# Last batch's norm woven into the batch ahead, VectorE for GpSimd at both ends of the second layer, sums on GpSimd in the third

## The reference, cut to what matters

```python
# second layer, end of a batch's block (b, l, e = 8, 256, 512); og is the result of the scan over l
m = og.mean(-1, keepdims=True)                       # per head of 16
va = ((og - m) ** 2).mean(-1, keepdims=True)
og = ((og - m) / jnp.sqrt(va + 1e-05)).reshape(b, l, e) * gn_w + gn_b
x1 = x + og * g @ Wo.T
xc = _ln(x1, ln2_w, ln2_b)
sx2 = jnp.concatenate([state[:, 0:1] - xc[:, :1], xc[:, :-1] - xc[:, 1:]], axis=1)
xk2 = xc + sx2 * ffn_maa_k
xr2 = xc + sx2 * ffn_maa_r
rr = jax.nn.sigmoid(xr2 @ Wfr.T)
kk = jnp.square(jax.nn.relu(xk2 @ Wfk.T))
return x1 + rr * (kk @ Wfv.T)

# third layer: two cross attentions (16 heads of 128), then the feed-forward part
h = _layer_norm(x, ln1_scale, ln1_offset)
x = res + _cross_attention(h, xf_1, wq1, ...)
h = _layer_norm(x, ln2_scale, ln2_offset)
x = res + _cross_attention(h, xf_2, wq2, ...)
h = _layer_norm(x, ln_mlp_scale, ln_mlp_offset)
h = gelu(h @ w_fc1 + b_fc1) @ w_fc2 + b_fc2          # inner width 2048
return x + h
```

## Time and profile before

| | |
|---|---|
| median of 3 runs (lowest to highest) | 4452.52 us (4450.16 to 4452.68) |
| the profiled execution: time, span | 4447.1 us, 4445.4 us |
| busy share of the span | TensorE 94%, VectorE 66%, ScalarE 44%, GpSimd 35% |
| mean granted TensorE clock | 0.98 of full |
| second layer | about 826 to 1829 us |
| third layer | about 1829 to 4366 us |

### The profile page before, as it was taken

One profiled execution on the slowest core, in us unless ns is written; L12 is line 12 of the kernel. 1 busy time (PEld: TensorE's weight loads), 2 busy tenths in 40 slices (PEclk: granted clock), 3 DMA queues, 4 the chain that ended last, 5 costly groups with the idle time before them and its releaser, 6 DMA issues. The chain is left out here.

```text
span 4445.4 us, 70612 instructions
## 1 busy us (share of the span) xinstructions
PE 4173.9 (94%) x22096; PEld 3147.2 (71%) x22096; DVE 2953.5 (66%) x6494; ACT 1964.5 (44%) x3814; POOL 1575.7 (35%) x1082
## 2 busy tenths in 40 slices
PE   7999999678999996699999999999999999999999
PEld 3444444356777774588887797887887977888866
DVE  5666665278888885375774775766776756757743
ACT  3555555222333321355553455552555543555522
POOL 1222333155566653123233333233332334232230
PEclk8999999899999998899999999999999999999999
DMA  1000000300000000222212322222212122222122
GB/s 40 25 22 28 20 20 15 119 5 10 15 15 15 15 10 19 84 63 77 68 58 74 96 65 77 63 72 71 92 59 76 58 73 92 64 86 65 54 79 97
DMA packets 128412, 239.78 MB, mean 54 GB/s; under 512 B 16932, under 2 KB 40100, under 8 KB 126896
## 3 DMA queue, kind: packets, MB, share of 16 engines
q1 hardware_dynamic: 126544, 232.99, 16.4%
q0 software_dynamic: 1008, 3.67, 0.2%
...
## 5 line engine op out<-in xcount | busy, mean ns | idle before, releaser
L1940 POOL TENSOR_TENSOR c_wl<-c_wr,c_wh 128x512 fp32r<-128x512 f32 (+1 forms) x576 | 819.7, 1434 | 1689.6 <-ACT c_wh L2273 1386.9
L2374 ACT ACTIVATE c_pr<-c_ps,c_nms 128x257 f32<-128x257 f32 x512 | 244.1, 477 | 483.8 <-DVE c_nms L2596 481.6
L582 ACT ACTIVATE a_ex<-a_ps 128x1024 f32<-128x1024 f32 x256 | 261.1, 1023 | 259.9 <-PE a_ps L417 259.8
L1529 DVE TENSOR_TENSOR_SCAN b_sb<-b_wt,b_s,b_ps 128x256 f32<-128x256 f32 x512 | 361.6, 736 | 16.3 <-PE b_ps L1072 4.4
L695 DVE TENSOR_REDUCE a_nm<-a_ps 128x2 f32<-128x1024 f32 x256 | 311.4, 1221 | 80.5 <-PE a_ps L394 80.4
L2273 ACT ACTIVATE c_wh<-c_wr 128x512 fp32r<-128x512 f32 (+1 forms) x464 | 315.4, 687 | 47.6 <-PE c_ps L2002 43.9
L1480 POOL TENSOR_TENSOR b_sb<-b_sb,b_rt 128x1024 f32<-128x1024 f32 x128 | 278.0, 2178 | 153.6 <-DVE b_sb L1529 113.3
L2000 PE MATMUL c_ps<-c_hh,c_wh 128*128 128x512 f32 x768 | 310.5, 404 | 12.5 <-DVE c_hl L2480 12.1
L2000 PE MATMUL c_ps<-c_gh,c_wh 128*128 128x512 f32 x768 | 307.5, 400 | 9.6 <-DVE c_gl L2658 4.3
L2002 PE MATMUL c_ps<-c_hh,c_wl 128*128 128x512 f32 x768 | 304.6, 397 | 0.0
L2001 PE MATMUL c_ps<-c_hl,c_wh 128*128 128x512 f32 x768 | 304.0, 396 | 0.0
...
## 6 DMA issues: line engine op xcount, KB each, us to landing
...
c_wr<-in_wk SPq DMA_DIRECT2D x128, 256.0 KB, 2.9
c_wr<-in_wq SPq DMA_DIRECT2D x128, 256.0 KB, 2.6
...
```

Of the source, the lines that this page charges most:

```text
L582: act.activation(EX[:, n % 4, :, :], ps[:, BT + 2 * (n % 2):BT + 2 * (n % 2) + 2, :], ACT.Exp).then_inc(ex_ready, 1)
L1529: mm = dve.tensor_tensor_scan(SB[:, quad % RING, pr % 2, e, 1:L + 1], WT[:, third(b, i), e, :], half(spread_bank(pair), e), S0[:, b % 2, 2 ...
L1940: pool.tensor_tensor(piece(WL, slot), piece(WR, slot), piece(WH, slot), ALU.subtract).then_inc(piece_cut[slot], 1)
L2374: act.activation(PR[:, i, 0:L + 1], ps[:, BS + 1 - i % 2, 0:L + 1], ACT.Exp, bias=NMS[:, i:i + 1], scale=float(K2) ** -0.5, accum_out=RS[: ...
```

## The change

Second layer, start (t = 0): `scale`, `shift` and the first `mix` addition go from GpSimd to VectorE, and `constants()` moves behind the reciprocal and the scaling. Second layer, end: `due_post` takes batch 7 out of `post_stage`, and of batch 6 the second `fr`, both `fv` and `out`. A function `last_stages` on TensorE, ScalarE and VectorE issues them: batch 7's group norm in turns with batch 6's remaining products, pairs in two banks (PA, PF, also GATHER and PB), gate, scaling and shift on VectorE, the residual taken from `XA` in place of a load into `XB`, and the output stored in two halves. Third layer: GpSimd adds the four chunks of x, and of the squares, of the woven norm, and TensorE multiplies the one sum; `variance` moves behind `up` of f=5; two of the down products move from ahead of head 15's scores to behind them.

```diff
         XK, XR, KK, TR, OUT = ZB, SQB, XPB[:, :, 0:L], SXB, ZB
+        ZL, XL = XF[:, 0], XA
         SELF = ZB[:, :, :].rearrange("p a (b m) -> p (a b) m", m=P)
         ps = stack.enter_context(nc.psum_tensor("b_ps", [P, 8, 512], F32))
         SPREAD, GATHER, PF, PA, PB = 0, 4, 5, 6, 7
+        LAST_BANKS, LAST_GATES = (PA, PF), (PB, PA)
 
...
+        def due_post(slot, first, last=B - 2):
+
+            s = due(slot, first)
+            return s if s is not None and s <= last else None
...
-            sp.wait_ge(out_stored, B * 16 + AHEAD)
+                    if post < B - 1:
+                        sp.dma_start(XB[:, :, :], x1T[post]).then_inc(res_in, 16)
+            for i in range(2):
+                pair = slice(2 * i, 2 * i + 2)
+                sp.wait_ge(out_ready, B + i + AHEAD)
+                sp.dma_start(x2T[B - 1][:, pair, :], OUT[:, pair, :]).then_inc(out_stored, 16)
+            sp.wait_ge(out_stored, (B + 1) * 16 + AHEAD)
...
-                    s = due(slot, PE_AT["gm"][i])
+                    s = due_post(slot, PE_AT["gm"][i])
...
-                    s = due(slot, PE_AT["fr"][i])
+                    s = due_post(slot, PE_AT["fr"][i], B - 2 - i)
...
-                    s = due(slot, PE_AT["fv"][i])
+                    s = due_post(slot, PE_AT["fv"][i], B - 3)
...
+            def last_stages():
+
+                r, s = B - 2, B - 1
+                pe.wait_ge(v_read, B * 2 + AHEAD)
+                pe.wait_ge(pa_read, B * UNITS + AHEAD)
+                pe.wait_ge(mix_read, B * 10 + AHEAD)
+                for i in range(2):
+                    pe.wait_ge(og_ready, s * 2 + i + 1 + AHEAD)
+                    for c in range(2 * i, 2 * i + 2):
+                        mm = pe.matmul(half(LAST_BANKS[i], c), BM[:, :], OG[:, s % 2, c, :], start=True, stop=True, skip_group_check=True)
+                    mm.then_inc(gm_ps, 1)
+                pe.wait_ge(tr_ready, r * 2 + 1 + AHEAD)
+                project(PB, W_FR, 1, XR).then_inc(fr_ps, 1)
+                pe.wait_ge(gq_ready, s + 1 + AHEAD)
+                pe.wait_ge(gc_ready, s * 2 + 2 + AHEAD)
+                for c in range(EC):
+                    mm = pe.matmul(half(PA, 0)[0:NH1, :], BMC[:, c, :], SQB[:, c, :], start=(c == 0), stop=(c == EC - 1), skip_group_check=True)
+                mm.then_inc(gv_ps, 1)
+                pe.wait_ge(kk_ready, (r + 1) * 2 + AHEAD)
+                project(GATHER, W_FV, 0, KK).then_inc(fv_ps, 1)
+                pe.wait_ge(gr_ready, s + 1 + AHEAD)
+                for i in range(2):
+                    for c in range(2 * i, 2 * i + 2):
+                        mm = pe.matmul(half(LAST_BANKS[i], c), BB[:, c, :], RS[:, :], start=True, stop=True, skip_group_check=True)
+                    mm.then_inc(bb_ps, 1)
+                pe.wait_ge(tr_ready, (r + 1) * 2 + AHEAD)
+                project(PB, W_FV, 1, KK).then_inc(fv_ps, 1)
+                pe.wait_ge(gated, s + 1 + AHEAD)
+                pe.wait_ge(gs_ready, s * 2 + 2 + AHEAD)
+                for i in range(2):
+                    project(LAST_BANKS[i], W_O, i, ZL).then_inc(wo_ps, 1)
+                pe.wait_ge(x1_ready, (s + 1) * 2 + AHEAD)
+                for k in range(EC):
+                    mm = pe.matmul(half(PA, 0), MEANW[:, :], XL[:, k, :], start=(k == 0), stop=(k == EC - 1), skip_group_check=True)
+                mm.then_inc(p_mean, 1)
+                pe.wait_ge(p_sq, s + 1 + AHEAD)
+                for k in range(EC):
+                    mm = pe.matmul(half(PF, 0), MEANW[:, :], SQB[:, k, :], start=(k == 0), stop=(k == EC - 1), skip_group_check=True)
+                mm.then_inc(p_var, 1)
+                pe.wait_ge(fk_in, s + 1 + AHEAD)
+                pe.wait_ge(p_sd, s + 1 + AHEAD)
+                for i in range(2):
+                    project(LAST_BANKS[i], W_FK, i, XK).then_inc(fk_ps, 1)
+                pe.wait_ge(fr_in, s + 1 + AHEAD)
+                pe.wait_ge(fv_read, (r + 1) * 2 + AHEAD)
+                for i in range(2):
+                    pe.wait_ge(kk_ready, s * 2 + i + AHEAD)
+                    project(LAST_GATES[i], W_FR, i, XR).then_inc(fr_ps, 1)
+                pe.wait_ge(kk_ready, (s + 1) * 2 + AHEAD)
+                project(PF, W_FV, 0, KK).then_inc(fv_ps, 1)
+                pe.wait_ge(tr_ready, s * 2 + 1 + AHEAD)
+                project(PB, W_FV, 1, KK).then_inc(fv_ps, 1)
...
+            def last_stages():
+
+                r, s = B - 2, B - 1
+                act.wait_ge(gc_ready, s * 2 + 2 + AHEAD)
+                act.wait_ge(fr_ps, (r + 1) * 2 + AHEAD)
+                act.activation(SQB[:, :, :], OG[:, s % 2], ACT.Square).then_inc(gq_ready, 1)
+                act.activation(TR[:, 2:4, :], both(PB), ACT.Tanh, scale=0.5).then_inc(tr_ready, 1)
+                act.wait_ge(gv_ps, s + 1 + AHEAD)
+                act.wait_ge(bb_ps, s * 2 + AHEAD)
+                act.activation(RS[0:NH1, :], half(PA, 0)[0:NH1, :], ACT.Sqrt, bias=EPS[0:NH1, 0:1]).then_inc(gd_ready, 1)
...
-                if t is not None:
+                if t is not None and t > 0:
...
                 t = due(slot, POOL_AT["shift"])
-                if t is not None:
+                if t is not None and t > 0:
...
-                    if t is not None:
+                    if t is not None and t + e > 0:
...
-                    if t == 0:
-                        constants()
                 t = due(slot, DVE_AT["inverse"])
                 if t is not None:
                     dve.wait_ge(a_sd, t + 1 + AHEAD)
                     dve.reciprocal(SDA[:, :], SDA[:, :]).then_inc(a_rs, 1)
+                    if t == 0:
+                        dve.drain()
+                        dve.tensor_tensor(XCA[:, :, :], XCA[:, :, :], SDA[:, :].unsqueeze(1).broadcast_to([P, EC, L]), ALU.mult).then_inc(a_xn, 1)
+                        constants()
                 t = due(slot, DVE_AT["blend"])
                 if t is not None:
+                    if t == 0:
+                        dve.wait_ge(a_xp, 1 + AHEAD)
+                        dve.tensor_tensor(SXA[:, :, :], XPA[:, :, 0:L], XPA[:, :, 1:L + 1], ALU.subtract).then_inc(a_sx, 1)
                     dve.wait_ge(a_sx, t + 1 + AHEAD)
                     dve.wait_ge(a_var, t + 1 + AHEAD)
                     for o in range(EC):
...
+                            if t + e == 0 and i == 1:
+                                dve.drain()
+                                dve.tensor_tensor(XF[:, 0], XF[:, 0], XPA[:, :, 1:L + 1], ALU.add).then_inc(xf_ready, 1)
...
+            def last_stages():
+
+                r, s = B - 2, B - 1
+                for i in range(2):
+                    dve.wait_ge(gm_ps, s * 2 + i + 1 + AHEAD)
+                    dve.tensor_tensor(OG[:, s % 2, 2 * i:2 * i + 2, :], OG[:, s % 2, 2 * i:2 * i + 2, :],
+                                      both(LAST_BANKS[i]), ALU.subtract).then_inc(gc_ready, 1)
+                dve.wait_ge(gd_ready, s + 1 + AHEAD)
+                dve.reciprocal(RS[0:NH1, :], RS[0:NH1, :]).then_inc(gr_ready, 1)
+                dve.wait_ge(fv_ps, r * 2 + 1 + AHEAD)
+                dve.wait_ge(tr_ready, (r + 1) * 2 + AHEAD)
+                dve.wait_ge(fk_ps, (r + 1) * 2 + AHEAD)
+                dve.scalar_tensor_tensor(OUT[:, 0:2, :], TR[:, 0:2, :], 1.0, both(GATHER), ALU.add, ALU.mult).then_inc(fv_read, 1)
+                for i in range(2):
+                    dve.wait_ge(bb_ps, s * 2 + i + 1 + AHEAD)
+                    dve.wait_ge(gq_ready, s + 1 + AHEAD)
+                    dve.tensor_tensor(OG[:, s % 2, 2 * i:2 * i + 2, :], OG[:, s % 2, 2 * i:2 * i + 2, :],
+                                      both(LAST_BANKS[i]), ALU.mult).then_inc(gs_ready, 1)
+                dve.wait_ge(gn_ready, s + 1 + AHEAD)
+                dve.wait_ge(gt_ready, s + 1 + AHEAD)
+                dve.wait_ge(pa_ps, B * UNITS + AHEAD)
+                dve.tensor_tensor(ZL, OG[:, s % 2], GT[:, s % 2], ALU.mult).then_inc(gated, 1)
+                dve.wait_ge(fv_ps, (r + 1) * 2 + AHEAD)
+                dve.scalar_tensor_tensor(OUT[:, 2:4, :], TR[:, 2:4, :], 1.0, both(PB), ALU.add, ALU.mult).then_inc(fv_read, 1)
+                dve.wait_ge(fv_read, (r + 1) * 2 + AHEAD)
+                dve.scalar_tensor_tensor(OUT[:, :, :], OUT[:, :, :], 0.5, XB[:, :, :], ALU.mult, ALU.add).then_inc(out_ready, 1)
+                for i in range(2):
+                    pair = slice(2 * i, 2 * i + 2)
+                    dve.wait_ge(wo_ps, s * 2 + i + 1 + AHEAD)
+                    dve.tensor_tensor(XL[:, pair, :], XL[:, pair, :], both(LAST_BANKS[i]), ALU.add).then_inc(x1_ready, 1)
...
+                dve.wait_ge(fk_ps, (s + 1) * 2 + AHEAD)
+                for i, bank in enumerate((PF, PB)):
+                    pair = slice(2 * i, 2 * i + 2)
+                    dve.wait_ge(fv_ps, s * 2 + i + 1 + AHEAD)
+                    dve.wait_ge(tr_ready, s * 2 + i + 1 + AHEAD)
```

(51 more changed lines are left out.)

105 lines of the change are left out of this document (72 added, 33 removed).

## The result

The changed kernel took 4406.06 us (median of four executions, 4405.52 to 4408.72), the one before on the same chip 4451.89 (4450.16 to 4452.68): a ratio of 0.9897, with a 95% interval of 0.9885 to 0.9908. Predicted were 4404.5, range 4392 to 4420.

The account below looks back on a forecast made before the run. Bound: TensorE in the third layer's feed-forward part, chains of short steps at the second layer's start and end. 6.0 + 27 + 15.5 - 0.5 = 48.0 off 4447.1 gives 4399.1; median 5.4 above, 4404.5; range 4392 to 4420.

Parts of the forecast that it names:

- Second layer, start: Batch 0's start: `hidden` 5.0 earlier and 1.0 from the first `mix` addition, 6.0 us saved (bounds 4.5 and 6.5).
- Second layer, end: Batch 7's norm to the last store: terms summing to 27.3, taken as 27 us saved (bounds 23 and 29.5).
- the whole layer moves with it: Second layer: the scan follows what TensorE delivers, so the start's 6.0 us would carry through the whole layer.
- the 2.7 of `wo` at full level: Second layer's end: `wo` would no longer start at the half level, 2.7 us saved.
- GpSimd's three steps: Second layer's end: gate on VectorE saves 1.1 us, `scale2` and `shift2` there save 1.8.
- the 2.40: Second layer's end: the wait of 2.40 us ahead of the variance would stay, saving 0.
- The rival of two thirds: Second layer's woven end gives two thirds, TensorE still at half level: 9 us less saved, 4413.5; 10%.
- Third layer, the sums: Feed-forward parts: GpSimd's sums spare twelve records of 0.43 in each of three norms, 15.5 us saved (bounds 15.5 and 0).
- the mechanism of the rival: Third layer: GpSimd's sums hold up VectorE, rounded activations come late and the sums give nothing, 4420 us; 8%.
- the 6 us of slack: Third layer's feed-forward part: 6 us left before a piece is needed, more than a GpSimd sum's 3.9.
- Moved down products: Third layer's head 15: TensorE's wait only moves ahead of the scores, 0.5 us lost (bounds 11 saved, 1.5 lost).
- The rival of 11 less: Third layer: the moved products fill TensorE's wait in eight attentions, 11 us more saved, 4393; 6%.

Follow-up runs that it names:

- before_again: The kernel before, unchanged, run again for a second profile: 4452.37 us, ratio 0.9999.
- after_again: The changed kernel, unchanged, run again: 4406.01 us, ratio 0.9893 to the kernel before.
- no_weave: The changed kernel with batch 6's last three product groups in front of batch 7's norm instead of inside it: 4420.3 us, ratio 0.9923.
- pool_end: The changed kernel with the second layer's last gate, scaling and shift back on GpSimd: 4409.75 us, ratio 0.9899.
- end_alone: Only the second layer's end (weave, banks, VectorE for GpSimd, output halves) on the kernel before: 4424.04 us, ratio 0.9935.
- after: The changed kernel with the whole change, against the kernel before: 4406.06 us, ratio 0.9897.
- no_moved: The changed kernel with the moved down products put back behind the scores of head 14 and 15: 4407.01 us, ratio 0.9895.

## Why the prediction was right, point by point

The time was right to 1.6 us. The saving was 48.0 by the prediction and 45.8 between the medians (46.4 in the second pair, `before_again` and `after_again`), so 2 too large. Between the profiled executions it was 40.8 and 42.2, since one execution lies up to 5 from its kernel's median: the first profile of before 4.8 below, that of `after_again` 4.0 above. So the 1.6 is in part luck; the stages can be checked only to a few us. By stage, from the table (us saved):

| stage | first pair | second pair | said |
|---|---|---|---|
| first layer | -3.2 | -1.9 | 0 |
| second layer up to the last `take_sums` | 2.7 | 2.8 | 6.0 |
| its end | 27.4 | 25.7 | 27 |
| third layer | 13.8 | 15.8 | 15.0 |
| fourth layer | 0.0 | -0.1 | 0 |

In both pairs the sum was too large at the same two places: the start, and the first layer, for which the prediction had no term.

- **Second layer, start: the steps right, the layer's share not.** Counted from the layer's first load, the mean of the six profiles has `hidden` 5.1 earlier (5.0 said) and `k` 5.5 (6.0 said), with the constants beside ScalarE's part as said. The step that failed is the last sentence, that "the whole layer moves with it": 3.1 of the 5.5 are left at the first `take_sums` and 2.2, less than the scatter, at the last. In the fill of the pipeline TensorE meets more work at its half level; that this is what gives the time back is argued from the windows and not shown, as no run took the half level away in that stretch alone.
- **Second layer, end: right.** 27 said, 27.4 between the first two profiles, 25.8 between the means, inside the bounds of 23 and 29.5. By terms: the weave is worth 7.2 by its order in `no_weave` (its cost inside the norm 3.3, where 2.7 and 1.0 were said), the 2.7 of `wo` at full level came as 2.8, GpSimd's three steps as 2.8 in `pool_end` (1.1 and 1.8 said) with 2.2 more by the clock that was not in the sum. Mean, variance and root kept their waits, the 2.40 with it. The rival of two thirds (18) fell with `end_alone`.
- **Third layer, the sums: right.** Each of the three feed-forward parts became shorter by 5.2 in every profile (5.2 said), 15.5 in all. The layer's total is 13.8 and 15.8 less between the two pairs, 13.3 on the mean, because the attentions scatter by some us without an edit to them: without the sums the layer takes 2531.0 to 2538.5. The first attention and the second one of the third pair became longer on the mean (268.1 to 270.1 and 264.6 to 266.9; four profiles without the sums, six with them). The first of these lies ahead of every sum, so waiting for a sum can't be its cause. In the second the changed kernel took 267.5 and `pool_end`, with the same third layer, 264.1, and TensorE's waits for VectorE's weights and rounded keys and queries add up to 6.0 there in the one and 3.2 in the other. What decides this stays open; no run settles whether the sums have a part in it.
- **GpSimd beside VectorE: the mechanism of the rival, without its consequence.** VectorE lost 3.5 per sum, and GpSimd's sum of squares took 4.6 in place of the 3.9 said:
```profile
2414.84 1.47 POOL L2123 TENSOR_TENSOR c_g<-c_g 128x512 f32<-128x512 f32 x1
2416.28 1.74 POOL L2124 TENSOR_TENSOR c_g<-c_g 128x512 f32<-128x512 f32 x1
2418.16 1.29 POOL L2126 TENSOR_TENSOR c_g<-c_g 128x512 f32<-128x512 f32 x1
```
 This is the exclusion that the Trainium skill describes (SBUF — State Buffer, "Who interferes with whom"), and the longer casts and subtractions agree with it. It didn't reach TensorE in the changed kernel: its waits in the first pair's part are the same as before, 1.7 us in three waits, the longest 0.7. That fits the 6 us of slack.
- **Moved down products: right in kind.** They moved part of the wait ahead of the scores and filled nothing (1.3 us of waits in the last head in place of 1.4). Between `after` and `no_moved` the 0.5 lost is 0 within 0.3. The rival of 11 less fell.
- **What would show it:** no GpSimd operation between the last gather and the third layer, `wo` at full level, two records each for mean and variance, no wait over 0.7, and the last store some 67.9 behind the norm's first matmul (67.8 said) all came, and the feed-forward part is 5.2 shorter. The clock times 848.2 and 859.7 did not, because the first layer ended 3.2 us later.
